# Six projections of a head pair in one visit of the attention loop, and the token and expert stages in one block whose first gathered rows are split by tiles

## The reference

```
q, k, v = einsum('bsm,hmd->bhsd', x, kernel[0..2])         # 16 heads of 64
attn = softmax(q k^T / (64*64*16)); out = (attn v) WO
x = layernorm(x + out)
probs = softmax(x gate_W); top 2 of 8 experts, weights to sum 1
out = 0.5 * gelu(x shared_W + shared_b)
out += combine[e] * (gelu(x W1[e] + b1[e]) W2[e] + b2[e])   # e = 0..7, hidden 1024
x = layernorm(x + layernorm(out) * gamma + beta)
```

## Time and profile before

| | us |
|---|---|
| median of 3 runs (lowest, highest) | 1801.71 (1800.16, 1803.23) |
| the profiled execution's own time | 1799.77 |
| its span in the trace | 1798.0 |

### The profile page before, as it was taken

How to read it: one execution, slowest core, us unless ns; L and a number is a source line. 1 busy time by engine, 2 the same in 40 slices (tenths; PEclk the granted TensorE clock), 3 DMA queues, 4 the chain that set the end, 5 groups by cost and what they waited for, 6 DMA issues and landing times. The chain is left out here.

```text
span 1798.0 us, 32053 instructions
## 1 busy us (share of the span) xinstructions
PE 1737.0 (97%) x11007; PEld 1201.3 (67%) x11007; DVE 1363.6 (76%) x2196; ACT 1035.7 (58%) x1529; POOL 399.3 (22%) x442
## 2 busy tenths in 40 slices
PE   9999999999999999999999999999779999999977
PEld 7555555555555555555555555799679999999972
DVE  6888888888888888788888889776656665565647
ACT  6555655655565565555556566476445555465537
POOL 1000000000000000000000000016756666677654
PEclk9999999999999999999999999999889999999998
DMA  5011111111111111311121111464223443334335
GB/s 182 31 36 48 36 36 42 36 36 36 48 36 36 42 36 42 118 51 36 36 88 36 42 36 36 149 204 152 96 80 90 90 90 89 48 90 90 88 66 168
DMA packets 80199, 127.12 MB, mean 71 GB/s; under 512 B 12752, under 2 KB 46736, under 8 KB 77776
## 3 DMA queue, kind: packets, MB, share of 16 engines
q1 hardware_dynamic: 61808, 98.27, 16.4%
q0 software_dynamic: 18272, 27.31, 7.7%
HBM read 86.72 MB, written 38.83 MB: 70 GB/s over the span
## 5 line engine op out<-in xcount | busy, mean ns | idle before, releaser
L533 ACT ACTIVATE a_e<-banks 128x1024 f32<-128x1024 f32 x512 | 483.2, 1030 | 192.6 <-PE banks L429 192.6
L649 DVE TENSOR_TENSOR a_esum<-a_esum,a_e 128x1024 f32<-128x1024 f32 x384 | 470.5, 1225 | 141.8 <-ACT a_e L533 108.3
L443 PE MATMUL banks<-a_e,a_v 128*64 128x512 f32 x2048 | 467.5, 598 | 0.0
L443 PEld LDWEIGHTS banks<-a_e,a_v 128*64 128x64 f32 x2048 | 135.5, 136 | 266.3 <-issue 242.6
L64 POOL MEMSET ident<- 128x128 f32 x1 | 0.2, 205 | 1118.8 <-POOLq L167 1118.8
L429 PE MATMUL banks<-a_qh,a_kh 64*128 64x512 f32 x1024 | 218.5, 420 | 2.6 <-DVE a_kl L586 1.6
L429 PE MATMUL banks<-a_qh,a_kl 64*128 64x512 f32 x1024 | 203.5, 390 | 0.0
L429 PE MATMUL banks<-a_ql,a_kh 64*128 64x512 f32 x1024 | 203.3, 390 | 0.0
L1884 ACT ACTIVATE e_g<-banks,e_b1c 128x256 f32<-128x256 f32 x280 | 115.7, 470 | 150.5 <-PE banks L1832 146.0
L429 PEld LDWEIGHTS banks<-a_qh,a_kh 64*128 64x128 f32 x1024 | 96.8, 183 | 110.9 <-issue 75.7
L1845 PE MATMUL banks<-woh,e_hh 128*128 128x256 f32 x560 | 162.3, 290 | 1.4 <-issue 0.2
(11 more groups left out here) (254 smaller groups left out, 3354.3 us busy)
## 6 DMA issues: line engine op xcount, KB each, us to landing
attn_out<-a_ot SPq DMA_DIRECT2D x64, 256.0 KB, 2.0
a_inv<-inv_rows SPq DMA_DIRECT2D x126, 128.0 KB, 2.8
a_w<-w_qkv SPq DMA_DIRECT2D x32, 256.0 KB, 3.1
raw<-attn_out SPq DMA_DIRECT2D x4, 2048.0 KB, 11.5
raw<-w_up SPq DMA_DIRECT2D x8, 1024.0 KB
raw<-w_down SPq DMA_DIRECT2D x8, 1024.0 KB
t_ot<-attn_out SPq DMA_DIRECT2D x3, 2048.0 KB, 9.9
raw<-x_t SPq DMA_DIRECT2D x8, 512.0 KB, 9.4
```

The costliest lines, as they stand in the source:

```text
L443: mm = pe.matmul(o_acc[h * DH:(h + 1) * DH, :], v[quad % 2][:, n, head], e[(slot * ST + n) % NE][:, h * BANK:(h + 1) * BANK], start=n == 0 ...
L533: act.activation(e[t % NE], ring[place(n) % RING], ACT.Exp, scale=SCALE).then_inc(e_ok, 1)
L649: dve.tensor_tensor(acc[:, :], acc[:, :], e[(slot * ST + n) % NE], ALU.add).then_inc(add_ok, 1)
```

## The change

In the attention loop the visit of slots with m = 0 is empty. The visit of slots with m = 1 holds all six units of the pair: Q and K of the first half, Q and K of the second half, two V tiles. The units use three banks in turn (`UNIT_BANKS`), so that the fourth unit waits until the first has been read out (for Q and K by DVE), the fifth for the second, the sixth for the third. Where a visit is empty its place in the ring of banks is left empty.

The token and expert stages become one block: `tokens` returns its bodies, `experts` calls each at the head of its own, and the barrier between them is gone. In its place each engine waits at the seam for the plan (`plan_ok`) and, on POOL and ACT, for the stores of the shared branch. The first gathered rows are handled in two parts: the first gather has a semaphore of its own, PE turns 128 rows into bank 4 and 128 rows into bank 5, and ACT and DVE make high and low parts of each half apart. Some semaphores are merged, and the load of the fourth part of the attention output waits for one tile more.

```diff
@@ units
             out = []
+            if m < NB - 1:
+                return out
             if i + 1 < B * PAIRS:
-                out += [(Q, i + 1, m), (K, i + 1, m)]
+                out += [(kind, i + 1, part) for part in range(NB) for kind in (Q, K)]
             if i // 4 + 1 < QUADS:
-                out.append((V, i // 4 + 1, i % 4 * NB + m))
+                out += [(V, i // 4 + 1, i % 4 * NB + part) for part in range(NB)]
             return out
+        UNIT_BANKS = 3
+        def units_in(slot, bank):
+            return [u for k, u in enumerate(units(slot)) if k % UNIT_BANKS == bank]
@@ unit_out
             slot, k = visit[u]
+            k = k % UNIT_BANKS
             return side if k == 2 else ring[HALF % RING][:, k * BANK:(k + 1) * BANK]
@@ pe_unit
-                if k < 2:
+                if k >= UNIT_BANKS:
+                    wait_evacuated(pe, units(slot)[k - UNIT_BANKS])
+                elif k < 2:
                     pe.wait_ge(e_ok, slot * ST + occupant(slot, HALF)[1] + 1)
-                elif slot and len(units(slot - 1)) > 2:
-                    wait_evacuated(pe, units(slot - 1)[2])
+                elif slot >= NB and units_in(slot - NB, 2):
+                    wait_evacuated(pe, units_in(slot - NB, 2)[-1])
@@ scores
                 held, tile_held = occupant(slot, place(n))
+                if held >= 0 and tile_held is None and not units(held):
+                    held, tile_held = occupant(held, HALF)
                 if held >= 0 and tile_held is None:
-                    for u in units(held)[0:2]:
+                    for u in units_in(held, 0) + units_in(held, 1):
                         wait_evacuated(pe, u)
@@ tokens, SP
-                    sp.wait_ge(otl_ok, HALF)
+                    sp.wait_ge(otl_ok, HALF + 1)
@@ tokens, POOL
-                  .then_inc(xg_in[0], 16)
-
-        @block.tensor
-        def _(pe):
+                  .then_inc(first_tile_in if a == 0 else xg_in[0], 16)
+            gp.wait_ge(plan_ok, 1)
+            gp.wait_ge(numbers_ok, 2)
+            stored_shared(gp)
+
+        def tensor(pe):
@@ experts, PE
-            pe.wait_ge(xg_in[0], 16 * CT)
-            turn_rows(0)
+            tokens_tensor(pe)
+            for a in range(CT):
+                if a == 0:
+                    pe.wait_ge(first_tile_in, 16)
+                else:
+                    pe.wait_ge(xg_in[0], 16)
+                for kk in range(KD):
+                    mm = pe.transpose(t_ps[a][:, kk * P:(kk + 1) * P],
+                                      xg[0][:, a, kk * P:(kk + 1) * P], ident[:, :])
+                mm.then_inc(turned if a else first_turned, 1)
@@ experts, ACT
-            rows_high(0, 0)
+            for a, (done, count) in enumerate(((first_turned, TT + 1), (turned, 1))):
+                act.wait_ge(done, count)
+                act.copy(xh[0][:, :, a * P:(a + 1) * P], rows_of(a)).then_inc(xh_ok if a else first_high_ok, 1)
@@ experts, DVE
-            rows_low(0, 0)
+            for a, (done, count) in enumerate(((first_high_ok, PARTS_SPLIT + 1), (xh_ok, 1))):
+                dve.wait_ge(done, count)
+                ins = dve.tensor_tensor(xl[0][:, :, a * P:(a + 1) * P], rows_of(a),
+                                        xh[0][:, :, a * P:(a + 1) * P].bitcast(F32), ALU.subtract)
+            ins.then_inc(xl_ok, 1)
```

More of the change, by code:

```diff
@@ L912, in _, with tokens @@
                 dve_general(dve)
-def tokens(nc, banks, keep, raw, x_rows, attn_out, x2_rows, acc_rows, w_rows, w_up, w_down, b_up, b2, beta):
+def tokens(nc, whole, banks, keep, raw, x_rows, attn_out, x2_rows, acc_rows, w_rows, w_up, w_down, b_up, b2, beta):
     x2, ident, numbers, plan, xg = (keep[n] for n in ("x2", "ident", "numbers", "plan", "xg"))
@@ L948, in sem @@
         def sem(name):
-            return ctx.enter_context(nc.semaphore(name))
+            return whole.enter_context(nc.semaphore(name))
         ahead_of = ahead(raw)
@@ L1053, in branched_before, with stored_shared, sync @@
             return [n for n in EARLY if EARLY[n] == t]
-        @block.sync
-        def _(sp):
+        def stored_shared(engine):
+            for u in range(2):
+                engine.wait_ge(shared_out[u], 16 * ((len(GROUPS) + 1 - u) // 2))
+        def sync(sp):
             load_rows(sp, keep, xr[1], x_rows, 1)
@@ L1077, in _, with gpsimd @@
                 sp.dma_start(to[:, :], whole[bass.ds(first_expert, 1)].rearrange("a p n -> p (a n)")).then_inc(done, 16)
-            sp.wait_ge(w_t_ok, 1)
+            sp.wait_ge(weights_ok, 2)
             sp.dma_start(w_rows, w_t[:, :]).then_inc(keep["w_out"], 16)
[L1080 to L1085, removed]
+        def gpsimd(gp):
             steps = [0]
@@ L1301, in _ @@
             act.wait_ge(gap_ok, 1)
-            act.activation(e2[:, :], gap[:, :], ACT.Exp).then_inc(e2_ok, 1)
+            act.activation(e2[:, :], gap[:, :], ACT.Exp).then_inc(weights_ok, 1)
             for part in range(len(SORTS)):
@@ L1310, in _, with vector @@
             act.wait_ge(w_turned, 1)
-            act.copy(w_t[:, :], banks[3][0:CH, 0:P]).then_inc(w_t_ok, 1)
-        @block.vector
-        def _(dve):
+            act.copy(w_t[:, :], banks[3][0:CH, 0:P]).then_inc(weights_ok, 1)
+            act.wait_ge(plan_ok, 1)
+            stored_shared(act)
+        def vector(dve):
             steps = [0]
@@ L1646, in outputs, with experts @@
     return sync, gpsimd, tensor, scalar, vector
-def experts(nc, banks, keep, w_up, w_down, x2_rows, acc_rows, w_rows, gamma, out):
+def experts(nc, banks, keep, begun, w_up, w_down, x2_rows, acc_rows, w_rows, gamma, out):
     x2, numbers, plan, w1, w1h, w1l, w2, b1all, b2all, beta_rows = (keep[n] for n in (
@@ L1698, in experts, with rows_count, rows_of @@
             nc, ctx, banks, keep, ident, all_stored, gamma, acc_rows, out)
+        tokens_sync, tokens_gpsimd, tokens_tensor, tokens_scalar, tokens_vector = begun
         block = ctx.enter_context(nc.Block())
         h_ps, t_ps, y_ps = banks[0:GROUPS], banks[GROUPS:GROUPS + 2], banks[GROUPS + 2:GROUPS + 4]
+        PARTS_SPLIT = 2
+        first_tile_in, first_turned, first_high_ok = (keep[n] for n in ("first_tile_in", "oth_ok", "woh_ok"))
+        def rows_count(u, chunks):
+            return 16 * CT * chunks - 16 if u == 0 else 16 * CT * chunks
+        def rows_of(a):
+            return t_ps[a][:, 0:KD * P].rearrange("p (k s) -> p k s", k=KD)
         w_flat = w_rows.rearrange("a p -> (a p)").unsqueeze(1)
@@ L1730, in _ @@
         def _(gp):
+            tokens_gpsimd(gp)
             prime(gp, y_stored)
@@ L1806, in end @@
                 sp.wait_ge(w2_in, 16 * (c + 1))
+            tokens_sync(sp)
             sp.wait_ge(w1h_ok, 1)
@@ L2009, in layer @@
         keep["xg"] = [ctx.enter_context(nc.sbuf_tensor(f"xg{u}", [P, CT, D], F32)) for u in range(2)]
-        tokens(nc, banks, keep, raw, x_rows, attn_out, x2_rows, acc_rows, w_rows, w_up, w_down, b_up, b2, beta)
+        begun = tokens(nc, ctx, banks, keep, raw, x_rows, attn_out, x2_rows, acc_rows, w_rows, w_up, w_down, b_up, b2, beta)
         take(ctx, (("shared", [P, TT, D], F32),))
-        experts(nc, banks, keep, w_up, w_down, x2_rows, acc_rows, w_rows, gamma, out)
+        experts(nc, banks, keep, begun, w_up, w_down, x2_rows, acc_rows, w_rows, gamma, out)
 def kernel(L0_attn_x, L0_attn_kernel, L0_attn_WO, L0_ffn_W1, L0_ffn_b1, L0_ffn_W2, L0_ffn_b2, L0_ffn_gate_W,
```

25 lines of the change are left out of this document (14 added, 11 removed).

## The result

| | before | changed |
|---|---|---|
| median of 14 runs each, us | 1803.23 (1800.16 to 1807.46) | 1808.93 (1804.47 to 1813.26) |
| ratio, 95% interval | | 1.0035 (1.0026 to 1.0043) |
| profiled execution, own time (span) | 1799.77 (1798.0) | 1804.47 (1802.7) |

The account below looks back on a forecast made before the run. PE was taken to bound attention, DVE having slack only in places. Attention +5.2 and seam -2.35 gave +2.9 on the profiled 1799.77, so 1802.7, and 1804.6 for the median; range 1798.5 to 1809.5.

Parts of the forecast that it names:

- Attention, forecast +5.2: Attention loop: merged visits' savings, waits and returned waits together make it 5.2 us longer.
- The visits' edges, 0.206 each: PE in attention: each of 31 visits removed saves 0.206 us at its two edges, 6.4 us in all.
- Rival 4: Attention: every change of tiling mode costs the same, so visits give 3.6 instead of 6.4; 1807.4 us; chance 0.08.
- DVE's arrival, 3.55 and 4.68: Merged visits: DVE's late arrival delays the fourth unit, 0.16 us in 23 plain pairs, 1.29 in six splitting x.
- Rival 1: Attention: DVE arrives by 3.39, the fourth unit doesn't wait, and the kernel is faster, 1795.7 us; chance 0.15.
- Pair 30 and slot 0, 0.7 and 1.1: Attention: pair 30 loses 0.7 us to the output weights' split, slot 0 loses 1.1 to the exponentials' pace.
- Given back, 1.6: Attention: waits behind late inverses in slot 41 (1.3 us) and for K's low part in slot 61 (0.29) vanish.
- Rival 2: Slot 41: early loads hold the inverses longer, so 1.3 isn't returned and up to 2.7 is lost; chance 0.14.
- The seam, forecast -2.35: Between tokens and experts: without the barrier and with halved rows, the first `up` starts 2.35 us earlier.
- The clock's rise: Start of `up`: PE's clock rise from half pace moves with its start; if it stays, 1.2 us is lost.
- Rival 3: The seam gives little, as rows arrive late or the clock rises later: 1.2 to 2.35 us lost; chance 0.13.
- Everything behind (weights, next rows) starts with it: Experts' stage: all work after the first `up` moves earlier with it, so the 2.35 us is kept.

Follow-up runs that it names:

- e3: Changed kernel with DVE's low parts of next weights and of x moved to the slot with m = 1, ACT's weight copy behind exponentials 4 to 7: 1783.06, ratio 0.9942.
- e4: Changed kernel with only DVE's low parts of rows of x moved to the slot with m = 1: 1788.68 us, ratio 0.9970 to the kernel before.
- e8: The kernel before, unchanged, measured again in a later batch without late signals: 1792.95 us.
- e5: The changed kernel, unchanged, measured again in a later batch without late signals: 1794.83 us, ratio 1.0008 to the kernel before.
- e9: The kernel before, unchanged, measured a third time, in a batch with late signals: 1804.67 us.
- e10: The changed kernel, unchanged, measured a third time, in a batch with late signals: 1809.70 us.
- e13: The kernel before with only the token and expert join and the split first gathers, visits as before: 1789.17 us, ratio 0.9990.
- e17: The kernel before with only the token and expert join and the split first gathers, repeated in another batch: 1790.82 us.

## Why the prediction was right and wrong

**Attention, forecast +5.2.** Right: 1108.9 to 1109.0 in six traces with merged visits as changed, 1103.4 to 1104.9 without, +4.8 between the means and +5.6 in the first pair.
- *The visits' edges, 0.206 each.* Held, by `e3`: 34.69 where 34.90 - 0.206 is 34.69. Rival 4, with 34.78, falls. The Trainium skill's page TensorEngine Tiling (Array Packing), Key Properties, says that a change of mode drains TensorE; it gives no price, and one price for every change is not what these rows show.
- *DVE's arrival, 3.55 and 4.68.* Measured 3.43 and 4.54 to 4.59 after the visit's start. The 0.12 less is as much as PE loses in the score group behind the missing visit, which moves the visit's start back. The prediction had that place and called it part of the 0.16, and the term holds: 0.19 a pair (34.88 - 34.69), 0.12 of it in the score group (3.10 against 2.98), behind ACT's copies, and 0.06 in the visit (8.44 against 8.38). Its sign, a wait of 0.1 at the fourth unit of plain pairs, left this out, and didn't show. The six pairs that split x take 36.02, 1.33 more than 34.69 for the forecast 1.29: 8.0 for 7.7. Of it `e4` gives 7.2 back. Rival 1 falls: arrival is 0.04 behind its point of 3.39, and its gain didn't come.
- *Pair 30 and slot 0, 0.7 and 1.1.* Waits of 0.47 and 0.86.
- *Given back, 1.6.* Held: no wait for inverses, slot 41 or later. Rival 2 falls. Slot 39 costs 0.27 more than a plain pair, which the sum doesn't have.

**The seam, forecast -2.35.** Right in size, 9.07 to 6.75, and 2.0 (`e8`, `e5`) and 2.2 (`e9`, `e10`) less in the later pairs. By parts: I gave the barrier 1.4 and the halves 0.95; they are 1.04 and 1.13, and 0.2 is a shorter second issue. The clock's rise did not simply move with the start. The granted clock is 0.50 in the window below and `up` runs at half pace until 1324.2, 4.2 behind its start (5.3 before), and `up` is 0.6 shorter, a gain that lies in the experts' stretch and that the sum doesn't have. Rival 3 falls.

```profile
1319.00:1324.00 5.00, 4.08 (x20) 4.03 (x20) 1.32 (x3) 4.15 (x4) 3.39 (x5) 0.50 0.14 40
```

The gather's 2.10 over a low part of weights was kept in the sum, and the measured 1.89 bears it out. In all twenty traces the issue that starts while DVE's low part (2.29) is running takes longer and ends after it: 1.8 to 2.1 as the second issue, ending 0.84 behind DVE, and 2.8 to 3.1 as the first, ending 0.95 behind. A first issue that began 0.01 to 0.38 before DVE's operation took 1.08, and DVE took its 2.29 to 2.31 all the same; free of it the second takes 0.97. The Trainium skill, SBUF — State Buffer, Who interferes with whom, has GpSimd wait for a port that it shares with DVE, and the trace agrees that it waits. The section also infers that a tensor_tensor doesn't hold up descriptor writing, though it contends with GpSimd's reads. These gathers read their row numbers from SBUF, so the rows don't tell whether the read or the writing waits; they show that the issue as a whole does.

**The step that failed: "Everything behind (weights, next rows) starts with it".** The sum has no term for the experts, which I took to be the same stretch, moved. In the first comparison it was 2.6 longer, and 2.5 in the second pair measured in that condition, and this makes the difference between the forecast 2.9 and the measured 5.7 (5.2 - 2.3 + 2.6 is 5.5). In place of "the same stretch, moved" the traces show PE standing still inside `up` for 6.7 us instead of 3.8, and 8.8 instead of 6.1, in batches in which its signals also come late. Without them the experts' stretch is 1.2 shorter (`e5` against `e8`), 0.7 of it in the first chunk, and the change costs 1.9 (ratio 1.0008).

What is shown: the place (inside `up`), the condition (two of six batches), and that late signals go with it. What stays open is the cause: why PE stops and its signals are late in some batches and not in others, and whether the change itself makes the stops longer. The chip's number doesn't decide the first: 0 stands at a batch without and at one with them. That the change does it is supported by two pairs, and by the whole time: it costs 4.7 to 7.8 in the first comparison and -0.2 to 3.2 in the later one. Against it stand the 2.8 and 2.9 by which one kernel differs from itself, and the equality under extra copies. So chance is not excluded, and neither edit was measured alone in that condition.

The chance of slower, 0.45, was put mostly on rivals 2, 3 and 4, of which none happened; that the measured time lies inside the range, at its upper end, is luck: the part above the forecast has a reason that the text didn't have.

## What to carry to other kernels

When work that was spread over two places is gathered in one, ask first which engine must have emptied the second half's buffers, and what that engine does just before. Here moving two DVE operations by one slot and an ACT copy behind the exponentials turned +5 us in attention into -8. An effect that two traces show in a stretch that the edit doesn't touch needs both kernels once more before it is explained. When an experiment's stretch starts with a software-issued transfer, count from the end of the issue.

## What was not expected of the hardware

- In the experts' stage of two of six batches, 12 to 16% of PE's recorded completion signals arrived over 0.5 us late, up to 3.3 us, and PE stood still inside rows of 48 matmuls without a wait, for up to 0.86 us at once and 3.8 to 8.8 us in all. In the other batches no recorded signal was over 0.02 us late, and `up` took 192.4 us for 34 chunks in each of fourteen traces. The stage takes 7 to 13 us more of 1800. No run shows the cause.
- A tensor_tensor of DVE with both inputs in SBUF holds up an indirect transfer's issue that starts under it until it is over (1.08 becomes 2.8 to 3.1, 0.97 becomes 1.8 to 2.1); one that began 0.01 to 0.38 us before it is not held up.
- The token stage takes 161.6 in one trace of the join alone (`e13`) and 166.8 in another (`e17`).
